# Query stacks copied one slot earlier, and all weights turned in one unrolled block

## The reference

```python
x = x + tanh(g_xattn[0]) * L0_xattn(layernorm(x), ctx, ctx)   # 16 heads of 16, "cope" positions
x = x + tanh(g_ffn[0])   * L0_ffn(layernorm(x))               # 8 experts, top 2, and a shared one
x = x + tanh(g_xattn[1]) * L1_xattn(layernorm(x), ctx)        # cross attention, 16 heads
x = x + tanh(g_ffn[1])   * L1_ffn(layernorm(x))               # gated self-attention, 16 heads
# the first attention ("core"):
gates = sigmoid(attn_logits)
pos = min(flip(cumsum(flip(gates))), npos_max - 1)
logits_int = einsum('bhqd,dn->bhqn', query, pos_emb)
scores = softmax(logits + logits_ceil * w + logits_floor * (1 - w))   # w = pos - floor(pos)
# an expert, for each token:
h1 = xt @ w1.T + b1;  h3 = xt @ w3.T + b3
y = swiglu(h1 * h3) @ w2.T + b2
```

## Time and profile before

| | |
|---|---|
| Time, median of 3 runs | 4901.44 us (4898.19 to 4908.12) |
| The profiled execution: its time, and its span in the trace | 4907.68 us, 4906.0 us |
| Busy: DVE, PE, ACT, POOL | 3975.6, 3332.2, 2426.4, 1394.9 us |
| Mean granted TensorE clock | 0.753 of full speed |

### The profile page before, as it was taken

One profiled execution on the slowest core, in us unless ns is written; L12 is line 12 of the kernel. 1 busy time (PEld: TensorE's weight loads), 2 busy tenths in 40 slices (PEclk: granted clock), 3 DMA queues, 4 the chain that ended last, 5 costly groups with the idle time before them and its releaser, 6 DMA issues.

```text
span 4906.0 us, 64542 instructions
## 1 busy us (share of the span) xinstructions
PE 3332.2 (68%) x21126; PEld 2210.1 (45%) x21126; DVE 3975.6 (81%) x8619; ACT 2426.4 (49%) x5505; POOL 1394.9 (28%) x1125
## 2 busy tenths in 40 slices
PE   3347677676767767676776767767676766767686
PEld 2125344453544436354453635435354443635363
DVE  3699787887978879787888978888797887978753
ACT  2464555545555454554545455554554545455432
POOL 0242322323232232322323232232323223232300
PEclk7558687686877778687786867778687777868687
DMA  4000000000000000000000000000000000000000
GB/s 130 13 5 1 1 12 1 11 1 1 12 1 12 1 11 1 1 12 1 11 1 3 10 1 12 1 11 1 1 12 1 12 1 11 1 1 7 1 7 3
DMA packets 42692, 40.93 MB, mean 8 GB/s; under 512 B 6469, under 2 KB 42343, under 8 KB 42361
## 3 DMA queue, kind: packets, MB, share of 16 engines
q1 hardware_dynamic: 42360, 36.85, 2.5%
HBM read 32.64 MB, written 4.19 MB: 8 GB/s over the span
## 4 chain that ended last, share of the span: by engine, by line
DVE 42%; PE 26%; ACT 13%; issue 13%; POOL 2%; DVEq 0%; POOLq 0%; ACTq 0%; DMA 0%; SPq 0%
DVE banks L731 7%; DVE u L962 5%; PE banks L288 4%; DVE row_negmax L1273 4%; PE banks L366 3%; PE banks L275 3%; DVE masks L722 3%; PE banks L297 3%; DVE eg_eth L980 3%; DVE c L689 3%; DVE o L989 2%; PE banks L330 2%; DVE steps L749 2%; PE banks L810 2%; ACT core_prob L581 2%
## 5 line engine op out<-in xcount | busy, mean ns | idle before, releaser
L731 DVE COPY_PREDICATED banks<-masks,banks 128x448 f32<-128x448 int16 (+5 forms) x1536 | 1030.6, 671 | 36.6
L632 POOL TENSOR_TENSOR steps<-slope,rises 128x512 f32<-128x512 f32 x256 | 301.3, 1177 | 2373.9 <-DVE masks L722 2162.0
L810 PE MATMUL banks<-xn,w 128*128 128x256 f16 x6912 | 876.7, 290 | 74.6 <-ACT h L882 50.0
L810 PEld LDWEIGHTS banks<-xn,w 128*128 128x128 f16 x6912 | 704.9, 104 | 239.4 <-ACT h L882 58.2
L689 DVE TENSOR_TENSOR_SCAN c<-gate,cap 128x514 f32<-128x514 f32 x256 | 371.0, 1449 | 83.6 <-POOL neg_rest L642 82.4
L1273 DVE TENSOR_REDUCE row_negmax<-banks 128x4 f32<-128x1024 f32 x256 | 297.3, 1216 | 154.5 <-PE banks L351 151.9
L722 DVE TENSOR_SCALAR masks<-shift 128x512 int16<-128x512 int16 x1536 | 334.3, 288 | 89.8 <-ACT shift L558 85.6
L823 PE MATMUL banks<-w,a 128*128 128x256 f32 x1152 | 303.6, 411 | 85.3 <-DVE o L989 79.0
L646 POOL TENSOR_TENSOR partial<-partial,core_scores 128x512 f32<-128x512 f32 x256 | 361.4, 1412 | 0.1
L642 POOL TENSOR_TENSOR neg_rest<-shift,c 128x512 f32<-128x512 bf16 x256 | 293.5, 1146 | 219.6 <-ACT shift L570 144.5
L882 ACT ACTIVATE h<-banks,b 128x256 f32<-128x256 f32 x576 | 239.8, 467 | 198.3 <-PE banks L810 197.3
(11 more groups left out here) (262 smaller groups left out, 7493.4 us busy)
## 6 DMA issues: line engine op xcount, KB each, us to landing
stage<-in_L_ffn_w SPq DMA_DIRECT2D x16, 512.0 KB, 5.5
ahead<-in_ctx SPq DMA_DIRECT2D x32, 128.0 KB, 2.2
ahead<-in_x SPq DMA_DIRECT2D x32, 128.0 KB, 2.3
u<-in_ctx SPq DMA_DIRECT2D x32, 128.0 KB
x<-in_x SPq DMA_DIRECT2D x32, 128.0 KB
out<-x SPq DMA_DIRECT2D x32, 128.0 KB, 1.8
stage<-in_L_ffn_w SPq DMA_DIRECT2D x8, 256.0 KB, 6.1
stage<-in_L_ffn_sw SPq DMA_DIRECT2D x2, 512.0 KB, 4.4
```

The source lines that it names most:

```text
L731: move = nc.vector.copy_predicated(tab[:, :, 0:S - b], k.masks[:, n, :, 0:S - b], tab[:, :, b:S])
L810: last = nc.tensor.matmul(k.bank[bank][:, f * S:(f + 1) * S], w[:, e, a, c, par, f * P:(f + 1) * P], k.x_parts[:, b, c, :], start=(n == 0) ...
```

## The change

It does three things.

1. In `PLAN` the piece "query stacks" of PE and ACT is taken as the last piece of the slot ahead of `MAXIMA` (one more L, slots 7 and 12 of a batch) and no more as the first F of `MAXIMA`. DVE and POOL have no instruction in that piece.
2. The loop over pairs of experts and the second call of `transpose_weights` become one call, written out: 26 blocks of attention weights and the shared expert in one first group, then four groups of 20. The tile `stage` grows from 26 to 86 blocks; loads of the last group reuse its places and wait for the transposes of their former contents.
3. The small loads are issued behind all weight loads of that one block.

Line numbers of the changed kernel are 2 higher in the main part.

```diff
--- before.py
+++ after.py
@@ -56,8 +56,9 @@
              "scores", "max_ready", "maxT_psum", "maxT_ready", "scoresT", "pT_ready", "pv_done",
        "oH_ready", "heads_psum", "o_ready", "oT_psum", "oT_ready", "y_done")
 LN = ("loads", "var_ready", "rstd_ready", "xn_ready", "xT_psum", "xT_ready")
-GROUP_LOADS = ("first_loads", "second_loads", "third_loads")
-SEMS = (["loads", *GROUP_LOADS, "stores", "transposed", "first", "evacuated", "consts", "step", "pool_step", "dve_core", "dve_side"]
+GROUP_LOADS = ("first_loads", "second_loads", "third_loads", "fourth_loads", "core_loads")
+STAGE = 86
+SEMS = (["loads", *GROUP_LOADS[:4], "stores", "transposed", "first", "evacuated", "consts", "step", "pool_step", "dve_core", "dve_side"]
         + ["core_" + n for n in LN + STACKS + (
             "ctxT_psum", "ctxT_ready", "k_psum", "v_psum", "v_ready", "q_psum", "q_ready",
             "offset_psum", "offset_ready", "scores", "scores_copied", "gates", "c", "shift", "shift_copied", "masks",
@@ -104,11 +105,11 @@
 LAG = 4
 AHEAD_PLACE = 3
 LATE = (10, 11)
-MAXIMA = (5 * "F" + 12 * "M" + 4 * "L", "0" + 8 * "4" + 12 * "5")
+MAXIMA = (4 * "F" + 12 * "M" + 4 * "L", "0" + 8 * "4" + 12 * "5")
 VALUES = (6 * "F" + 5 * "L", 11 * "5")
 PLAN = [("FMM", "346"), ("FFML", "245"), ("FFL", "135"), ("FFL", "135"), ("FFL", "135"), ("FFML", "1245"),
-        ("FFL", "1245"), ("FFML", "1346"), MAXIMA, VALUES, ("FFFML", "00066"),
-        ("FFMM", "0346"), ("FMM", "046"), MAXIMA, VALUES, ("FFFML", "00066"), ("FF", "13")]
+        ("FFL", "1245"), ("FFMLL", "1346"), MAXIMA, VALUES, ("FFFML", "00066"),
+        ("FFMM", "0346"), ("FMML", "046"), MAXIMA, VALUES, ("FFFML", "00066"), ("FF", "13")]
 AHEAD = [1, 1, 1, 1, 1, 1, 0, 0, 2, 1, 1, 1, 2, 1, 1, 1]
 G = B * H
 SLOTS = G + H + LAG + 1
@@ -176,7 +177,7 @@
     return step
 
 
-def transpose_weights(nc, k, groups, small_loads=()):
+def transpose_weights(nc, k, groups, small_loads):
 
 
 
@@ -195,13 +196,15 @@
             for g, group in enumerate(groups):
                 for src, destinations, _ in group:
                     rows = len(destinations)
-                    sp.dma_start(k.stage[:, n:n + rows, :], src.rearrange("(r p) n -> p r n", p=P))\
+                    at = n % STAGE
+                    if n >= STAGE:
+                        sp.wait_ge(sem["transposed"], n + rows - STAGE)
+                    sp.dma_start(k.stage[:, at:at + rows, :], src.rearrange("(r p) n -> p r n", p=P))\
                         .then_inc(sem[GROUP_LOADS[g]], 16)
                     n += rows
             for dst, src in small_loads:
                 sp.dma_start(dst, src).then_inc(sem["loads"], 16)
-            if small_loads:
-                sp.wait_ge(sem["loads"], 16 * len(small_loads))
+            sp.wait_ge(sem["loads"], 16 * len(small_loads))
 
         @block.tensor
         def _(pe):
@@ -212,7 +215,7 @@
                     pe.wait_ge(sem["evacuated"], n - 7)
                 for c in range(NC):
                     last = nc.tensor.transpose(k.bank[n % 8][:, c * P:(c + 1) * P],
-                                               k.stage[:, n, c * P:(c + 1) * P], k.ident[:])
+                                               k.stage[:, n % STAGE, c * P:(c + 1) * P], k.ident[:])
                 last.then_inc(sem["transposed"], 1)
 
         def source(n):
@@ -221,7 +224,6 @@
 
         @block.scalar
         def _(act):
-
             for n, (dst, view) in enumerate(blocks):
                 if view == "parity":
                     act.wait_ge(sem["transposed"], n + 1)
@@ -1483,7 +1485,7 @@
         preamble = ctx.enter_context(ExitStack())
         k.stack = preamble
         k.temp_tmp = sb("temp_tmp", [P, 3, H])
-        k.stage = sb("stage", [P, 26, D])
+        k.stage = sb("stage", [P, STAGE, D])
         k.bias_rows = sb("bias_rows", [NE, 2, 2 * F])
         k.small_rows = sb("small_rows", [32, D])
         k.emb = sb("emb", [P, NPOS + 1])
@@ -1575,13 +1577,10 @@
             return group
 
         flat = "e r n -> (e r) n"
-        with nc.Fori(0, E // 2) as e:
-            transpose_weights(nc, k, [expert_group(w1[bass.ds(i, 1)].rearrange(flat),
-                                                   w3[bass.ds(i, 1)].rearrange(flat),
-                                                   w2[bass.ds(i, 1)].rearrange(flat), bass.ds(i, 1))
-                                      for i in (e * 2, e * 2 + 1)])
-
-
+        experts = [expert_group(w1[i:i + 1].rearrange(flat), w3[i:i + 1].rearrange(flat),
+                                w2[i:i + 1].rearrange(flat), slice(i, i + 1)) for i in range(E)]
+        experts = [experts[i] + experts[i + 1] for i in range(0, E, 2)] 
+        shared = expert_group(sw1, sw3, sw2, slice(E, NE))
         row = lambda a: a.rearrange("(o n) -> o n", o=1)
         columns = lambda dst, a: [(dst[:, g:g + 1], a[g * P:(g + 1) * P].rearrange("(p o) -> p o", o=1))
                                   for g in range(NC)]
@@ -1612,7 +1611,7 @@
         plain = [[(src, [dst[:, :, r * P:(r + 1) * P] for r in range(D // P)], "plain") for dst, src in some]
                  for some in (((k.wq_cope, Wq0), (k.wk_cope, Wk0), (k.wv_cope, Wv0), (k.wo_cope, Wo0)),
                               ((k.wq_gated, Wq2), (k.wk_gated, Wk2), (k.wv_gated, Wv2), (k.wo_gated, Wp2)))]
-        transpose_weights(nc, k, [expert_group(sw1, sw3, sw2, slice(E, NE))] + plain, small)
+        transpose_weights(nc, k, [plain[0] + plain[1] + shared] + experts, small)
         with nc.Block() as block:
             @block.scalar
             def _(act):
```

## The result

| | before | changed |
|---|---|---|
| median of the runs, us | 4904.8 (4898.2 to 4910.1, 4 runs) | 4841.1 (4839.7 to 4844.3, 4 runs) |
| profiled execution: time, span, us | 4907.7, 4906.0 | 4840.3, 4838.6 |
| ratio of the changed kernel to before | | 0.9871, 95% interval 0.9855 to 0.9886 |

The change takes 63.7 us off; 69 were forecast. So the forecast's 4832 lies between two measurements of one kernel. Single executions differ by more than the 0.1% named ahead of the prediction: before's 11 in the first session of experiments lie between 4895.0 and 4927.0, 0.65% apart.

The account below looks back on a forecast made before the run. The main part was taken as a relay with DVE in most legs, the preamble as stages behind barriers. 50.4 (weights) plus 18.5 (slots), 69 us, off the profiled 4907.7 gave 4839, a median of 4832; range 4808 to 4857.

Parts of the forecast that it names:

- The weights' block, 50.4 forecast: Preamble: with all weights in one block, the following block starts at 64.3 us instead of 114.7, 50.4 us less.
- hence done by some 28: Preamble: SP's 35 weight issues, about 0.5 us each, are finished by some 28 us, small loads' issues by about 50.
- bound below: Preamble: if SP's outstanding loads are limited to 2.4 MB, the next block starts at 70.3 us and only 44 are saved.
- if SP's small issues end after 63: Preamble: stated sign that the weights' forecast is wrong; the small issues were expected to take until about 50 us.
- The cross slot, 1.0 forecast: Cross attention's maxima: transposes start 1.0 us earlier and DVE's wait moves between second and third reduce; 15 us over fifteen slots.
- The gated slot, 0.25 forecast: Gated attention's maxima: transposes start at 2360.22 instead of 2360.50, about 0.25 us gained; 3.5 us over 14 slots.
- first pair 0.64 later: Gated slot: ACT waits for PE's first pair, taken as 0.64 us, so its copies run from 2353.85 to 2356.65.
- rival 4: Maxima slots: ACT waits for PE, so exponentials, transposes and third reduce come later; slots lose 68 us, time 4919; chance 0.03.
- The sum of the main part, 18.5 forecast: Main part: 15 us from fifteen cross attention slots and 3.5 from 14 gated ones, 18.5 us in all.
- 7 us either way: Main part: allowance for TensorE's granted clock; a high clock alone was put at 7.5 us more, time 4824.
- DVE gains its whole wait: Maxima slots: DVE's whole shift comes through, all 82 us, time 4769; chance 0.07.
- late instructions: Preamble's written-out block: instruction fetches stand behind queued weights and DVE ends at 75.3 instead of 62.7, time 4845; chance 0.10.

Follow-up runs that it names:

- the gated part alone: Changed kernel with the cross attention's query stacks as in before, only the gated attention's moved: 4852.1 us, ratio 0.9890.
- the block alone: Changed kernel with before's `PLAN` and `MAXIMA`, so only the weights' block and the small loads' order are changed: 4863.0 us, ratio 0.9898.
- eight heads first: Changed kernel with PE's scores of heads 1 to 8, not 4 heads, ahead of the `core_prob` transposes in `MAXIMA`: 4783.0 us, again 4783.5.
- the second measurement: The changed kernel, unaltered, measured again in the second session beside before at 4908.2: 4825.6 us, ratio 0.9834.
- the cross attention alone: Changed kernel with query stacks moved only for the cross attention, the gated attention's pieces as in before: 4833.2 us, ratio 0.9843.
- the small loads between the groups: Changed kernel with tiny small loads issued ten at a time behind each of the first four weight groups: 4825.8 us; with eight heads' scores first 4786.4.

## Why the prediction was right, and where it was off

**The weights' block, 50.4 forecast, 43.2 in the trace.** Gains by mechanism came as said: no loop barriers, no landings without work, DVE busy from 23.4 to 64.2. Two steps were off. The first data was used at 22.64 instead of 21.9, as the rate starts lower than behind before's barrier (260 GB/s from 12 to 15, against 369 from 86 to 89 in before; why isn't shown), and DVE ended at 64.2 instead of 62.7. The other is larger. The step that failed is "hence done by some 28": the sum took every issue at 0.5 us and hid the small loads' 22 us behind DVE. SP was held until 46.92, so the small issues ended at 68.58 and the block started 2.9 us behind them. That is the forecast's own "bound below", whose condition was "where SP cannot have more loads outstanding than the trace shows"; it gave 70.3 us, and 71.5 were measured. It had put 2.4 MB as outstanding; 1.7 were. The forecast's own sign of being wrong on the weights, "if SP's small issues end after 63", came. The reason given against the bound, "no row shows SP held up by a full queue", was hasty. These are rows of before, the last weight load and the stretch of all eleven:

```profile
88.78 0.72 SPq L198 DMA_DIRECT2D stage<-in_L_ffn_Wp  x1
83.68:89.54 5.86, 0.00 (x0) 0.00 (x0) 0.00 (x0) 0.00 (x0) 0.00 (x0) 0.52 0.75 252
```

The seven loads of the same size ahead of it took 0.47 us each, and the first small issue behind it took 0.69, where the same instruction took 0.41 in the changed kernel. By 89.54 some 1.5 MB of the 3.4 had moved, so 1.9 MB were outstanding and not 2.4. Short signs, but they pointed at the limit.

**The cross slot, 1.0 forecast, 1.06 by medians.** Right with its mechanism: waits of 3.7 and 2.5 us at the first and third reduce, PE at the transposes for `core_prob`, and 2.6 us more as soon as the transposes stood behind head 8. PE waits 2.33 us at the transposes, as the forecast said it would.

**The gated slot, 0.25 forecast, a loss of 0.07.** The term that was off is the distance from PE's first pair to ACT's copy, "first pair 0.64 later": it is 1.06 (2294.55 to 2295.61). 0.64 was the distance between two other instructions of the cross slot, ACT's copy of one pair and PE's start of the next, and doesn't hold the pair's own matmuls, which take 1.04 us for two pairs. The forecast's times have 0.68 between the two (2353.17 to 2353.85) and a gain of 0.28 (2360.22 instead of 2360.50); 0.38 more makes a loss of 0.10 of it, and 0.07 were measured. This is rival 4's mechanism, ACT waiting for PE and the exponentials coming later, at a small size. The run with the gated part alone shows what it is worth: nothing.

**The sum of the main part, 18.5 forecast, more measured.** The cross move is worth 30 us against the block alone. By the slots' sums the changed kernel gained 1.6 and 2.5 us a batch in its two traces, times 15 some 24 and 38, and 16 of it are the 1.06 in 15 slots. The rest lies in slots 10, 11 and 15 and in single long forms of slot 8, each 0.2 to 0.7 us shorter by its mean; slot 0 gives 0.4 back. The forecast had no term for other slots; it allowed "7 us either way" for TensorE's clock, too little. The short forms of slot 15 are more frequent in most kernels that have the moved copies of the cross attention than in those that don't; with eight heads first they nearly vanish. Some of them run at a high granted clock and others don't, so the clock is a companion and not a shown cause. What picks the forms was not isolated, and the cause of this part of the gain stays open.

**The rivals.** That DVE gains its whole wait (4769) was excluded by the second wait, which took another edit to remove (4783). Nothing stood for late instructions: DVE has no gap between 23.4 and 64.2 in the written-out block, with the queues full. That the slots gain nothing, a slower kernel, and no effect at all: none happened. The two errors, 7 us too much in the block and 6 to 20 too little in the slots, have opposite signs, which is why the sum was nearer than its terms. In the profiled execution they nearly cancel, 67.4 us off where 69 were forecast. That is luck: in the second measurement, with the block's error the same, 82.6 came off.

**The range.** Its lower end doesn't follow from its own words: half of the way from 4832 down to 4769 is 31.5 us and not 24, so the range should have begun at 4800. The measured 4841 lies inside either.

## What to carry to other kernels

A queue that is kept full holds the engine that issues: cost a long row of loads at the rate of its data, not at the price of an issue, and ask what must still be issued behind it. Filling the issuer's waiting time with other small issues starved the data here, where the queue held 5 us of it; longer pieces (2 to 4 KB for each partition in place of 1 KB) helped twice, in rate and in depth. Issuing the small loads from another engine was not tried. Where a wait is moved and not removed, look for the instruction that now stands in front of the waited-for work, and move the work ahead of it: here that was worth 50 us in the first session (against the cross attention alone) and 39 in the second (4825.8 to 4786.4, both with the small loads between the groups), with one line of a table; the change itself had gained 16 in these slots.

## What the runs showed of the hardware that was not expected

- SP's queue took in about 1.7 MB of 1 KB pieces and 4.4 MB of 2 to 4 KB pieces before it held the issuing engine; nearer to a count of pieces than of bytes or of loads.
- Loads in 1 KB pieces ran at 348 GB/s in before (88 to 95 us) and at 349 in the changed kernel, the same bytes in 2 to 4 KB pieces at 404. The forecast weighed the Trainium skill ("DMA: Bandwidth & Descriptors", section Bandwidth), which measured 341 GB/s for 1 MB and 425 for 16 MB; here it was the pieces' length that moved the rate, with 13.9 MB in either case.
- Strided writes of VectorE (every second element of rows of f32 weights) cost nothing: 0.74 us for two evictions of 128x256 with them and 0.75 without.
- The changed kernel's two measurements, each beside before, gave ratios of 0.9871 and 0.9834, whose intervals don't meet. What moves one kernel by 0.4% between two sessions isn't known, so a difference of that size between sessions is no finding.
